# Cross scores of batch 1 in a six-layer stage: every second tile written to the banks of the transposed scores and of the weighted sums

## The reference, cut to what matters

```python
NL, D, H, DFF = (6, 128, 16, 512)
HD = D // H                                   # 8
for i in range(NL):
    xn = _adaln(x, noise_emb, n1_w[i], n1_b[i])
    ...
    a = _attn(q, k, v, src_mask).reshape(B, L, D) @ so_w[i].T
    x = x + a
    xn = _adaln(x, noise_emb, n2_w[i], n2_b[i])
    q = _rope((xn @ cq_w[i].T).reshape(B, L, H, HD))
    k = _rope((context @ ck_w[i].T).reshape(B, LC, H, HD))
    v = (context @ cv_w[i].T).reshape(B, LC, H, HD)
    a = _attn(q, k, v, ctx_mask).reshape(B, L, D) @ co_w[i].T
    x = x + a
    xn = _adaln(x, noise_emb, n3_w[i], n3_b[i])
    h = jax.nn.gelu(xn @ f1_w[i].T + f1_b[i], approximate=False)
    x = x + (h @ f2_w[i].T + f2_b[i])
```

## Time and profile before

| | |
|---|---|
| median of three runs | 2681.18 us (2678.3 to 2685.4) |
| the profiled execution, its own time | 2693.05 us |
| span of its trace | 2691.2 us |
| TensorE busy / VectorE / ScalarE | 2259.9 / 1687.6 / 1132.4 us |
| mean granted TensorE clock | 0.912 |
| VectorE's maxima of the self scores, L2392 | 768 of 685 ns, 184.2 us idle before them |
| VectorE's maxima of the cross scores, L2486 | 192 of 471 ns, 61.4 us idle before them |
| TensorE's cross scores, L1863 | 384 of 589 ns, 41.2 us idle before them |

### The profile page before, as it was taken

How to read it: one execution, slowest core, us unless ns; L and a number is a source line. 1 busy time by engine, 2 the same in 40 slices (tenths; PEclk the granted TensorE clock), 3 DMA queues, 4 the chain that set the end, 5 groups by cost and what they waited for, 6 DMA issues and landing times.

```text
span 2691.2 us, 32165 instructions
## 1 busy us (share of the span) xinstructions
PE 2259.9 (84%) x11288; PEld 897.5 (33%) x11288; DVE 1687.6 (63%) x3866; ACT 1132.4 (42%) x1855; POOL 142.9 (5%) x143
## 2 busy tenths in 40 slices
PE   5999969789999598887788688788878869877898
PEld 2333334343333275223222232322322233232433
DVE  4666648546565567775675577568467657745464
ACT  1333323102222133465466366456636636653321
POOL 0000000011111030000000000000000000010000
PEclk8999979859999699799798799889979989988999
DMA  3000000030000011000010010001001000020000
GB/s 141 1 1 0 1 0 1 3 107 1 1 1 1 12 41 42 5 21 2 24 41 1 24 41 2 24 1 42 1 24 41 2 24 4 22 99 0 1 0 8
DMA packets 38033, 54.34 MB, mean 20 GB/s; under 512 B 5073, under 2 KB 34546, under 8 KB 36338
## 3 DMA queue, kind: packets, MB, share of 16 engines
q1 hardware_dynamic: 37874, 52.28, 6.2%
HBM read 32.34 MB, written 0.52 MB: 12 GB/s over the span
## 4 chain that ended last, share of the span: by engine, by line
PE 38%; DVE 10%; ACT 7%; issue 4%; SPq 0%; DMA 0%; ACTq 0%; DVEq 0%
PE ps L1762 7%; PE ps L1744 5%; ACT big L2220 4%; PE ps L1725 4%; DVE C_nm L2392 4%; PE ps L1807 2%; PE ps L1886 2%; PE ps L1993 2%; PE ps L1898 2%; PE ps L1989 2%; PE ps L2014 2%; PE ps L1905 2%; PE ps L1863 2%; ACT big L2300 2%; PE ps L1914 2%
## 5 line engine op out<-in xcount | busy, mean ns | idle before, releaser
L2392 DVE TENSOR_REDUCE C_nm<-ps 128x1 f32<-128x512 f32 x768 | 501.1, 685 | 184.2 <-PE ps L1725 180.4
L2220 ACT ACTIVATE big<-ps 128x512 f32<-128x512 f32 x768 | 427.8, 596 | 235.6 <-PE ps L1744 226.3
L1725 PE MATMUL ps<-C_attn 62*128 62x512 bf16 x768 | 277.6, 418 | 57.9 <-DVE C_nm L2392 47.0
L1744 PE MATMUL ps<-C_attn 64*128 64x512 bf16 x768 | 253.4, 398 | 62.3 <-ACT big L2220 51.7
L1762 PE MATMUL ps<-big,C_attn 128*32 128x512 f32 x1536 | 213.8, 630 | 13.3 <-ACT big L2220 13.3
L1725 PEld LDWEIGHTS ps<-C_attn 62*128 62x128 bf16 x768 | 63.6, 94 | 304.6 <-DVE C_nm L2392 158.8
L713 DVE TENSOR_REDUCE A_nm<-ps 128x2 f32<-128x1024 f32 x64 | 77.5, 1212 | 117.2 <-PE ps L500 117.1
L1744 PEld LDWEIGHTS ps<-C_attn 64*128 64x128 bf16 x768 | 59.2, 93 | 274.5 <-ACT big L2220 203.1
L2300 ACT ACTIVATE big<-ps,C_biasx 77x512 f32<-77x512 f32 x192 | 115.5, 678 | 55.9 <-PE ps L1890 55.8
L2486 DVE TENSOR_REDUCE C_nmx<-ps 128x4 f32<-128x308 f32 x192 | 78.5, 471 | 61.4 <-PE ps L1867 61.2
L650 ACT ACTIVATE A_p<-ps 128x1024 f32<-128x1024 f32 x64 | 65.6, 1025 | 112.6 <-PE ps L528 112.6
(11 more groups left out here) (379 smaller groups left out, 3817.6 us busy)
## 6 DMA issues: line engine op xcount, KB each, us to landing
C_attn<-C_first SPq DMA_DIRECT2D x144, 128.0 KB, 2.4
C_w<-in_C_w SPq DMA_DIRECT2D x6, 1090.0 KB, 5.1
C_attn<-in_D_ew SPq DMA_DIRECT2D x4, 1536.0 KB, 10.2
big<-in_B_ew SPq DMA_DIRECT2D x8, 514.0 KB
normw_later<-in_norm_w SPq DMA_DIRECT2D x1, 2304.0 KB, 15.8
A_w<-in_A_w SPq DMA_DIRECT2D x2, 1024.0 KB, 9.2
A_w<-in_A_w SPq DMA_DIRECT2D x2, 768.0 KB, 5.6
B_w<-in_B_w SPq DMA_DIRECT2D x1, 1536.0 KB, 11.1
```

Source lines behind the costliest of these rows:

```text
L1725: pe.matmul(ps[:, bank, :], lhsT=qs[side(hp, MAX_ROW), b, 2 * q + pq, t * P:(t + 1) * P], rhs=ks[side(hp, MAX_ROW), b, 2 * q + pq, :], sta ...
L1744: pe.matmul(ps[:, bank, :], lhsT=ks[side(1 - hp, HALF), b, 2 * q + pq, kt * P:(kt + 1) * P], rhs=qs[side(1 - hp, HALF), b, 2 * q + pq, :], ...
L2220: act.activation(prob[:, kt % 2, pq, 1 - hp, :], ps[:, bank, :], ACT.Exp, scale=SCALE)\
L2392: dve.tensor_reduce(nm[:, q % 2, t, pq, hp:hp + 1], ps[:, bank, :], AX.X, ALU.max, negate=True).then_inc(emptied[bank], 1)
```

## The change

In every odd unit but the last (units 1, 3, 5, 7 and 9) cross tiles 1 and 3 take banks 2, 3 and 4 and one of the ring, where they took banks 0 and 1 and two of the ring. Ahead of the `take`s stands a wait for the copy of the unit's own last weighted sums (`cw_ready`), and the first `weigh` of the next unit waits until bank 4 has been read out. No instruction is added, removed or moved.

```diff
+def turns_aside(n, t):
+
+    return n % B == 1 and t % 2 == 1 and n < UNITS - 1
+
...
                     if n == 0 and g == 0:
                         for k in range(2):
                             drained(pe, ("down_b", B * E_MOE - 1 - k))
+                    if g == 0 and n and turns_aside(n - 1, TB - 1):
+                        drained(pe, ("sx", n - 1, TB - 1, 2))
                     if g == 0:
                         pe.wait_ge(va_ready, (n + 1) * (TB - 1))
...
                     if t == 0:
                         pe.wait_ge(kc_ready, 4 * (layer(c) + 1))
                         pe.wait_ge(qx_ready, c + 1)
-                    banks = [take(("sx", c, t, r), S_BANK + r) for r in range(fixed(c))]
-                    banks += [fill(("sx", c, t, r)) for r in range(fixed(c), 4)]
+                    if turns_aside(c, t):
+                        pe.wait_ge(cw_ready, (c + 1) * QUADS)
+                        banks = [take(("sx", c, t, r), ST_BANK + r) for r in range(3)]
+                    else:
+                        banks = [take(("sx", c, t, r), S_BANK + r) for r in range(fixed(c))]
+                    banks += [fill(("sx", c, t, r)) for r in range(len(banks), 4)]
```

## The result

| | before | after |
|---|---|---|
| median of six runs | 2682.17 us (2678.3 to 2685.4) | 2669.19 us (2665.99 to 2673.17) |
| ratio, with its 95% interval | | 0.9947 (0.9929 to 0.9965) |
| profiled execution | 2693.05 us | 2668.63 us |
| span of the trace | 2691.2 us | 2666.8 us |

The change makes the kernel 0.5% faster, 13 us. The forecast was 2660 us, 22 us less than before, with a range of 2646 to 2672. So the direction is right, the range holds it, and 8 or 9 us of the forecast gain are missing.

What follows compares the result with a forecast made beforehand. The kernel is bound by a chain of hand-overs, no engine busy throughout. Five units x 4.2 us gave 21 us, taking the median from 2681.18 to 2660 us; range 2646 to 2672 with rival 1 and part of rival 2.

Steps and rivals of the forecast that it cites:

- The chain lies in the tiles of the odd units: Odd units' cross tiles: TensorE's matmuls and VectorE's maxima alternate on the chain; unit 5, 1739.98 to 1753.14.
- Tile 1 starts behind tile 0: Banks free, so no wait for maxima; VectorE goes on 2.56 us after tile 0's start (T), not 3.97: 1.41 us gained.
- Tile 2 at T+2.70, read from T+4.36: Cross tile 2, T being tile 0's start: waits for tile 0's fourth maximum; 2.66 us gained so far.
- The self scores: Two self scores between tiles 2 and 3: banks back at T+4.9 and T+5.3, scores ready by T+6.0, read until T+7.21.
- rival 2: Half of it: tile 1 not behind tile 0, or late copies holding the first self score; 9 us, 2672; chance 0.08.
- Tile 3 read from T+7.4, 4.2 us gained: Last cross tile, held only by TensorE's order: read at T+7.4 instead of T+11.61; bounds 4.0 to 4.56 us a unit.
- Added waits at nothing: The 15 added waits are for work ended long before, costing nothing; at 0.13 us each, 2 us in all.
- So the 4.2 us are passed on: Behind tile 3: everything later hangs on VectorE's end of tile 3, so each odd unit keeps its 4.2 us gain.
- the term of the clock: Shifted low-clock stretches: plus or minus 1.4 us a unit, 7 us in all, with no sign.
- Rival 1, the clock stays up: From tile 1 on, TensorE stays busy and the low stretch shrinks: 6.2 us a unit, 31 us, 2650; chance 0.15.
- The report of the Trainium skill: Double-buffering PSUM gained nothing where matmuls already ran together; by it near 0, 2681 us. The prediction sided against it.
- Rival 4: Slower: behind tile 3, shifted work hits low-clock stretches more often, losing over 5.8 us a unit; 2690; chance 0.03.

Runs made afterwards that it cites:

- Each half alone: The change with only cross tile 1 aside, or only tile 3: tile 1 alone took 2682.7 to 2663.4 us; tile 3 alone brought nothing that can be told.
- held: The change, with VectorE taking tile 3's first three maxima twice, once into a scratch tile, in the five odd units: 2655 us, ratio interval 0.9884 to 0.9925.
- filled_late: The change plus four unread matmuls around the transposed cross scores behind tile 3 of the odd units: time within the interval of `filled_more`.
- ring_kept_late: `ring_kept` plus the four unread matmuls of `filled_late`: missed its expected 2645 to 2652 us by 16 us.
- filled_more: `filled_late` plus five more unread matmuls ahead of the second weighted sums of the odd units: ratio 0.9887, 2654 us.
- ring_kept: The change, but each tile aside also skips one turn of the ring, so later steps keep their earlier ring bank: 2655 us.
- takes_apart: The change, but each bank's wait stands ahead of its own matmul, not all four ahead of the first: 2.5 us under the change, not told from it.

## Why the prediction was right or wrong

- **The chain lies in the tiles of the odd units:** right. Each half alone moved the turn by what its own steps gave, tile 3 to within 0.4 us.
- **Tile 1 starts behind tile 0:** right; its matmuls start 0.73 us after tile 0's in all five units.
- **Tile 2 at T+2.70, read from T+4.36:** right to 0.01 us.
- **The self scores:** TensorE starts them at T+4.98, worked out T+4.9, in four units. In unit 5 the weights for the first of them show the copies as their last releaser (the row at 1730.67), yet they start at T+4.95 as in the others. In unit 7 the copies did hold it (the row at 1956.84): tile 3's matmuls started 0.24 us later and the turn came 0.25 us later. That is the second shape of rival 2, and one of the signs that the prediction named for being wrong; it came true in one unit of five, at that price.
- **Tile 3 read from T+7.4, 4.2 us gained:** read from T+7.50, and the turn 4.12 us earlier (3.85 in unit 7). Right.
- **Added waits at nothing:** right as far as the trace shows; no wait of the change is on the chain.
- **"So the 4.2 us are passed on":** the step that failed, together with its correction, plus or minus 1.4 us a unit "with no sign". The order of work behind the tiles is passed on, its duration isn't: it took 1.76 us more in the mean, of one sign in four units and zero in one. I had priced the clock from the spread of two units of the kernel before and taken the five units as independent. I had also read only the first low stretch of unit 5, 17.15 us, against one of 23.9 in unit 3, and not the second of 10.24 that follows it. But low stretches begin at nearly the same place behind T in every unit (1.8 to 2.3 us before, 1.9 to 2.5 after), so a shift of 4.1 us can do the same to most of them. The mechanism of the gain was right and the term of the clock mis-sized: 0, with 7 us to either side, in place of 8.8 us in this pair of traces. The range, which had room for more than the clock, held the total all the same.
- **Rival 1, the clock stays up:** no. With the change it fell at T+2, as before; made to stay up to T+5.4, it gave 0.72 us a unit at the tiles and not the 6.2. The Trainium skill, "TensorE: Matmul & The Clock Gate", "A second HAM failure mode: psum-queue depth-cycling", says that waits for banks make the clock swing. Here TensorE's idle time from T to the turn fell from 6.1 us (14.56 less 8.43 busy) to 3.5 us (10.44 less 6.90), and the low stretch began at the same place and was longer; so fewer such waits did not bring the clock back in these runs, and whether the rest of them keep it swinging is not shown.
- **The report of the Trainium skill**, "TensorE: Matmul & The Clock Gate", "HAM oscillation — how this bites in real kernels", that double-buffering PSUM brought nothing further, does not carry over to this chain: VectorE's waits for the tiles went from 5.6 to 1.6 us and the kernel became faster.
- **Rival 4** named the place where the gain was partly lost, behind the turn, and its mechanism. It was priced too far away to be taken into the sum.

What stays open: why the clock comes back at T+16, T+22.6 or T+29.4. The runs show that it depends on when TensorE's work comes and where its gaps are (`held`, `filled_late`), not a rule by which to forecast the next one; `ring_kept_late` was forecast by such a rule and missed. Between the best four kernels (`filled_more`, `held`, `ring_kept`, `filled_late`) no order is shown.

## What to carry to other kernels

A chain that alternates between two engines over a few banks is worth breaking wherever other banks lie idle, and the local gain could here be worked out to 0.1 us from the rows. Whether it reaches the end depends on what the shift does to the clock behind it: look at how the low stretches lie to the unit, and where they begin at the same place in each, give the clock's term a sign and the number of units, not a spread. Where a gain falls short, delay the same chain by a microsecond, or fill TensorE's gaps, before looking for another wait.

## What the runs showed of the hardware that was not expected

- Adding 1.15 us of work to the chain of each of five units made the kernel 14 us faster (2669 to 2655). The granted clock came back at T+22.8 or earlier in three of the five units of its trace.
- TensorE was busy throughout for 11.61 us at 1.2 GHz (the second of the two rows of unit 5 after the change) before the clock came back; four matmuls that compute nothing, in two gaps of 0.8 us ahead of that, brought it back at T+15.6 instead of T+29.5.
- Over 70 units a microsecond more at the low level goes with 0.27 us more time, not half a microsecond. TensorE has 38% of the chain on the page; that this is why is argued, not shown.
- One and the same sequence of instructions took 119.32 us and 126.49 us in two units of one execution.
- Copies that landed 1 to 2 us late in single units delayed the turn there, by 0.25 us (the row at 1956.84) and by 1 us (the row at 1958.82). In these two units the low stretch ended at T+15.6 (a second one followed) and T+22.4, and not at T+29; in two units of `takes_apart` with late copies it still ended at T+29.6 and T+30.6.
